# TensorE takes the six row products of a convolution two at a time, between the three chunks of direct rows

## The chip, the cores and the metric

The kernel runs on one core of a Trainium2 chip. The metric is the device time of one execution in microseconds (us); the kernel before has a median of 1493.2 us over 3 runs (1492.6 to 1494.61).

## What is computed

A residual block with batch normalisation over the whole batch, on 32 images of 128 channels and 56 x 56 pixels, in float32:

```python
residual = x
out = conv3x3_decomposed(x, lsq_quantize(w1, alpha1))
out = jax.nn.relu(batchnorm(out, gamma1, beta1))
out = conv3x3_decomposed(out, lsq_quantize(w2, alpha2))
out = batchnorm(out, gamma2, beta2)
out = jax.nn.relu(out + residual)
```

The convolutions are 3 x 3 with padding 1. `lsq_quantize` rounds the weights to integers from -4 to 3 times a scale. Mean and variance of a batch normalisation are taken over all images, so the second convolution can't start before the first has gone through all of them.

## The kernel before

**Phases.** The 128 channels lie on the 128 partitions. Phase 1 convolves the 32 images with w1 and sums their values and squares; phase 2 applies the first normalisation and ReLU, convolves with w2 and sums again; the last phase adds the residual, applies the second normalisation and ReLU and stores. Ten images fit in SBUF (`slots`); the others go out to HBM and come back. A step g is one image in phase 1 (g = 0 to 31) or phase 2 (g = 32 to 63).

**One image.** Output rows 0 to 35 are made by a Winograd scheme in the vertical direction: nine tiles of four rows, each from six sums of input rows. DVE makes these sums (`v_rows`, lines 619 to 639, by way of `q_rows` and `p_rows`), and they are split in a high and a low part (`v_hi`, `v_lo`), which TensorE multiplies one after the other. The six products of an image, here p0 to p5, are six matmuls of 512 columns each (line 855; three horizontal taps times two parts), each into a PSUM bank of its own (0 to 5). Output rows 36 to 55 are made directly: three chunks, here c0, c1 and c2, of 7, 7 and 6 rows, 18 matmuls each (line 875) of 398 columns in c0 and c1, and of 342 or 284 in c2. They read `d_hi` and `d_lo`, the two parts of the input rows from 35 on. c0 and c2 share PSUM bank 6, c1 has bank 7.

**The engines around TensorE, in the order of their own programs.** Every engine runs its instructions in the order written, and waits on semaphores.

- ACT, function `step` (line 497), for image g: `hi_direct` (462) makes `d_hi` of image g, once all three chunks of image g-1 are done, since they read the plane it writes; `take_chunk` (476) takes c2 of image g-1 out of PSUM; `take_m` (470) copies p0, then later p2 of image g; three squares (488) of image g-1; `hi_pairs` (457) makes `v_hi` of image g+1 in three pairs, pair k once p(2k+1) of image g is done (the wait in line 456); in phase 2 only, two ReLU instructions (494) on image g+2; `take_chunk` of c0 and of c1 of image g.
- DVE, function `step` (line 707): `make_qp(g+1)` (622, 623); `lo_direct` (648), which makes `d_lo` of image g from `d_hi`; `make_v(g+1)` (626 to 639); the sums of products (659 to 671) with `lo_of_pair(g+1, 0)` (643) among them; `rows_out` (673 to 692), whose row 3 waits for all six products; `add_totals` (697).
- POOL, `lo_of_pairs` (line 415): `v_lo` of pairs 1 and 2 (418), each when ACT has made its `v_hi`.
- TensorE, `convolve` (line 881): `products` waits for `v_lo` (lines 840, 844, 846) and for the DVE work that frees each bank. `chunk` waits, for c0, for `d_lo` of this image (line 866) and for all chunks of the image before to be out of PSUM (868); for c2, that c0 of this image is out of bank 6:

```python
if j == 2:
    pe.wait_ge(evac_done, g * NC + 1)
```

- SP issues loads and stores. At the end of phase 2 it also loads the first residual images into `xbuf`, the fourth and fifth (line 374 ff.) when the last image's six products are done, since their places hold what the products read.

`m_done` counts products, `chunk_done` chunks, `evac_done` chunks that are out of PSUM, `hi_ready` and `lo_ready` / `pool_lo_ready` the parts.

Of the kernel before, what the change touches and what calls it, by code (L numbers as in the profile page):

```python
# [27 lines left out]
def residual_block(nc, x, w1, alpha1, gamma1, beta1, w2, alpha2, gamma2, beta2, out):  # L28
# [13 lines left out]
    M = 6  # L42
# [34 lines left out]
    with ExitStack() as ctx:  # L77
# [131 lines left out]
        def run(plane, r0, r1, shift):  # L209
            at = LEAD + r0 * PITCH + shift  # L210
            return plane[:, at:at + run_length(r1 - r0)]

        def bank_run(bank, rows):
            return psum[:, bank, 0:run_length(rows)]
# [16 lines left out]
        def w_bank(k, h):  # L231
            return psum[:, W_BANK[k] + h, :].bitcast(BF16)
# [593 lines left out]
        @block.tensor  # L826
        def _(pe):
            def transpose_weights(k):
                pe.wait_ge(w_int_ready[k], 1)
                for h, (first, end) in enumerate(W_LOTS):  # L830
                    for t in range(first, end):
                        last = nc.tensor.transpose(w_bank(k, h)[:, (t - first) * C:(t - first + 1) * C],
                                                   w_int[k][:, t * C:(t + 1) * C], ident[:, :])
                    last.then_inc(transposed, 1)

            def products(g, w):
                first_step = isinstance(g, int) and g == 0
                for k in range(M):
                    if k == 0:
                        pe.wait_ge(lo_ready, g * LO + 1)  # L840
                        if not first_step:
                            pe.wait_ge(m_copied, g * 2 - 1)
                    if k == 2:
                        pe.wait_ge(pool_lo_ready, g * PLO + 1)
                    if k == 4:
                        pe.wait_ge(pool_lo_ready, g * PLO + 2)
                    if not first_step:

                        if k in (1, 2, 3):
                            pe.wait_ge(sums_ready, g * SR - (0, 4, 1, 0)[k])  # L850
                        if k in (4, 5):
                            pe.wait_ge(rows_ready, g * RR - (k - 4))
                    for kw in range(3):
                        for half in range(2):
                            last = nc.tensor.matmul(bank_run(M_BANK[k], TILES),  # L855
                                                    w[:, M_WEIGHT[k] + kw, :],
                                                    run(v_plane[half], k * TILES, (k + 1) * TILES, kw - 1),
                                                    start=(kw == 0 and half == 0), stop=(kw == 2 and half == 1))
                    last.then_inc(m_done, 1)


            taps = sorted(((kh, kw) for kh in range(3) for kw in range(3)), key=lambda t: t != (1, 1))

            def chunk(g, j, w):
                if j == 0:
                    pe.wait_ge(lo_ready, g * LO + LO)
                    if not (isinstance(g, int) and g == 0):
                        pe.wait_ge(evac_done, g * NC)
                if j == 2:
                    pe.wait_ge(evac_done, g * NC + 1)  # L870
                for n, (kh, kw) in enumerate(taps):
                    r0 = CHUNKS[j][0] + kh - 1
                    r1 = min(H, CHUNKS[j][1] + kh - 1)
                    for half in range(2):
                        last = nc.tensor.matmul(bank_run(CHUNK_BANK[j], r1 - r0),  # L875
                                                w[:, kh * 3 + kw, :],
                                                run(d_plane[half], r0 - WINO + 1, r1 - WINO + 1, kw - 1),
                                                start=(n == 0 and half == 0), stop=(n == TAPS - 1 and half == 1))
                last.then_inc(chunk_done, 1)

            def convolve(g, w):
                products(g, w)
                for j in range(NC):
                    chunk(g, j, w)

            pe.wait_ge(ident_ready, 1)
            transpose_weights(0)
            pe.wait_ge(wT_ready, 6)
            pe.wait_ge(pads_ready, PADS)
            for n in range(5):  # L890
                convolve(n, wT[0])
            pe.wait_ge(m_copied, 5 * 2)
            pe.wait_ge(sums_ready, 5 * SR - 1)
            transpose_weights(1)
            pe.wait_ge(wT_ready, 2 * 6)
            convolve(5, wT[0])
            with pe.Fori(3, IMAGES // 2) as i:
                for b in range(2):
                    convolve(i * 2 + b, wT[0])
            convolve(IMAGES, wT[1])  # L900
            convolve(IMAGES + 1, wT[1])
            with pe.Fori(IMAGES // 2 + 1, IMAGES) as i:
                for b in range(2):
                    convolve(i * 2 + b, wT[1])
# [21 lines left out]
```

## Time and profile before

| | |
|---|---|
| median of 3 runs | 1493.2 us (1492.6 to 1494.61) |
| profiled execution | 1492.18 us, of which the span is 1490.3 us |
| TensorE busy | 1134.6 us (76% of the span) |
| DVE busy | 1128.4 us (76%) |
| ACT busy | 854.7 us (57%) |
| POOL busy | 298.5 us (20%) |
| phase 1, first to last product | 24.0 to 587.2 us |
| phase 2, first to last product | 615.1 to 1169.8 us |
| last phase | from about 1187 us |

The span is from the first to the last instruction of one profiled execution; 1.9 us of its time lie outside it. Busy shares are means over three phases with different limits, so a stage has to be read by itself: how far one engine is from full in an image of phase 1 or 2, and which wait ends last there. A matmul's listed duration includes the time it takes to run through the array, so neighbouring rows overlap; what one costs is the distance of two starts.

### The profile page before, as it was taken

What the parts mean: (1) busy time and instruction counts of PE and PEld (TensorE: products, weight loads), DVE (VectorE), ACT (ScalarE), POOL (GpSimd) and SP (SyncE); (2) the same over time, 40 slices, a digit from 0 to 9 for tenths busy, and PEclk for the clock granted to TensorE, in tenths of its full rate; (3) what the DMA queues carried; (4) which work ended last, traced back from release to release, by engine and by line L of the source; (5) the groups of instructions that cost most, each with busy time, mean ns of one, the idle gap of its engine ahead of it and who ended that gap; (6) DMA issues with size and microseconds to landing.
All of it is one profiled execution on the core that took longest, in us unless ns stands there. A gap on an engine that the chain in (4) does not pass through costs nothing.

```text
span 1490.3 us, 18967 instructions
## 1 busy us (share of the span) xinstructions
PE 1134.6 (76%) x5802; PEld 1031.6 (69%) x5802; DVE 1128.4 (76%) x1626; ACT 854.7 (57%) x1263; POOL 298.5 (20%) x147
## 2 busy tenths in 40 slices
PE   3999999999999999599999999999999600000000
PEld 2998999999999999499999999999999600000000
DVE  7998888888888885798888888888888452322324
ACT  3555555555665554677777777777777352222234
POOL 3222222222222221322222222222222000000000
PEclk9999999999999999799999999999999855555555
DMA  4354555444442210022244555444230699999999
GB/s 164 135 197 151 193 188 195 190 172 172 172 179 108 101 43 0 1 87 87 86 172 183 194 188 195 188 172 172 86 129 33 231 414 431 430 429 429 430 430 408
DMA packets 28101, 296.88 MB, mean 199 GB/s; under 512 B 3888, under 2 KB 3888, under 8 KB 4784
## 3 DMA queue, kind: packets, MB, share of 16 engines
q1 hardware_dynamic: 22608, 245.25, 41.7%
q10 hardware_dynamic: 5472, 51.38, 8.1%
q8 instruction: 9, 0.15, 0.0%
q14 instruction: 12, 0.10, 0.0%
HBM read 174.59 MB, written 122.03 MB: 199 GB/s over the span
## 4 chain that ended last, share of the span: by engine, by line
issue 65%; DMA 17%; POOL 14%; DVE 1%; ACT 1%; POOLq 1%; ACTq 0%; DVEq 0%
POOL v_lo L418 14%; DMA slots<-conv_spill 11%; DMA out<-slots 4%; DMA xbuf<-in_x 3%; DVE slots L821 1%; ACT slots L576 1%; POOLq L423 0%; POOLq L417 0%; POOLq L77 0%; POOLq L418 0%; ACTq L580 0%; DVE tiny L748 0%; DVE affine L750 0%; DVE affine L751 0%; POOL ident L404 0%
## 5 line engine op out<-in xcount | busy, mean ns | idle before, releaser
L418 POOL TENSOR_TENSOR v_lo<-v_rows,v_hi 128x1008 fp32r<-128x1008 f32 x128 | 296.2, 2334 | 831.2 <-ACT v_hi L457 831.2
L875 PE MATMUL conv_psum<-d_hi,w1T 128*128 128x398 f32 (+2 forms) x864 | 284.6, 333 | 0.0
L875 PE MATMUL conv_psum<-d_hi,w2T 128*128 128x398 f32 (+2 forms) x864 | 284.6, 333 | 0.0
L875 PE MATMUL conv_psum<-d_lo,w1T 128*128 128x398 f32 (+2 forms) x864 | 283.3, 332 | 0.0
L875 PE MATMUL conv_psum<-d_lo,w2T 128*128 128x398 f32 (+2 forms) x864 | 283.3, 332 | 0.0
L855 PE MATMUL conv_psum<-v_hi,w2T 128*128 128x512 f32 x576 | 227.9, 396 | 18.3 <-DVE v_lo L643 18.3
L855 PE MATMUL conv_psum<-v_hi,w1T 128*128 128x512 f32 x576 | 229.2, 398 | 10.4 <-DVE v_lo L643 5.5
L488 ACT ACTIVATE squares<-slots,minus_shift 128x1008 bf16 (+3 forms) x192 | 225.0, 1172 | 8.4 <-ACT squares L488 2.9
L855 PE MATMUL conv_psum<-v_lo,w1T 128*128 128x512 f32 x576 | 229.2, 398 | 0.0
L855 PE MATMUL conv_psum<-v_lo,w2T 128*128 128x512 f32 x576 | 228.2, 396 | 0.0
L821 DVE SCALAR_TENSOR_TENSOR slots<-slots,affine,xbuf 128x3136 f32<-128x3136 f32 (+1 forms) x30 | 97.4, 3265 | 151.1 <-DMA slots<-conv_spill 146.9
L576 ACT ACTIVATE slots<-slots,affine 128x3136 f32<-128x3136 f32 (+1 forms) x34 | 93.6, 2754 | 202.8 <-DVE slots L821 202.0
L476 ACT ACTIVATE slots<-conv_psum 128x392 f32 (+3 forms) x192 | 91.5, 476 | 194.9 <-PE conv_psum L875 194.9
L457 ACT CAST v_hi<-v_rows 128x1008 fp32r<-128x1008 f32 x192 | 185.9, 1029 | 9.6 <-DVE v_rows L630 6.5
L648 DVE TENSOR_TENSOR d_lo<-slots,d_hi 128x1176 fp32r<-128x1176 f32 x64 | 88.6, 1385 | 125.1 <-ACT d_hi L462 125.1
L875 PEld LDWEIGHTS conv_psum<-d_lo,w1T 128*128 128x128 f32 x864 | 162.8, 188 | 1.3
L875 PEld LDWEIGHTS conv_psum<-d_lo,w2T 128*128 128x128 f32 x864 | 162.8, 188 | 1.3
L875 PEld LDWEIGHTS conv_psum<-d_hi,w2T 128*128 128x128 f32 x864 | 162.4, 188 | 1.4
L875 PEld LDWEIGHTS conv_psum<-d_hi,w1T 128*128 128x128 f32 x864 | 162.4, 188 | 1.3
L462 ACT CAST d_hi<-slots 128x1176 fp32r (+1 forms) x64 | 75.5, 1180 | 131.4 <-PE conv_psum L875 131.4
L606 DVE SCALAR_TENSOR_TENSOR q_rows<-slots 128x2016 f32 (+1 forms) x64 | 144.2, 2253 | 4.2 <-ACT slots L494 4.2
L855 PEld LDWEIGHTS conv_psum<-v_hi,w2T 128*128 128x128 f32 x576 | 109.1, 189 | 42.2 <-DVE v_lo L643 18.5
(75 smaller groups left out, 1509.0 us busy)
## 6 DMA issues: line engine op xcount, KB each, us to landing
conv_spill<-slots SPq DMA_DIRECT2D x44, 1568.0 KB, 6.1
slots<-conv_spill SPq DMA_DIRECT2D x44, 1568.0 KB, 10.9
slots<-in_x SPq DMA_DIRECT2D x31, 1568.0 KB, 8.9
out<-slots ACTq DMA_DIRECT2D x30, 1568.0 KB, 11.5
xbuf<-in_x SPq DMA_DIRECT2D x28, 1568.0 KB, 52.1
xbuf_w<-in_x SPq DMA_DIRECT2D x4, 1568.0 KB, 51.9
out<-slots ACTq DMA_DIRECT2D x4, 784.0 KB, 10.8
slots<-in_L_conv_w SPq DMA_DIRECT2D x2, 576.0 KB, 9.8
```

What stands on the lines that cost most here:

```text
L418: nc.gpsimd.tensor_tensor(pair_window(1, k), pair_rows(k), pair_window(0, k).bitcast(F32), ALU.subtract).then_inc(pool_lo_ready, 1)
L457: nc.scalar.copy(pair_window(0, k), pair_rows(k)).then_inc(hi_ready, 1)
L462: nc.scalar.copy(window(d_plane[0], 0, D_ROWS), rows_of(slot(p + SLOTS, WINO - 1))).then_inc(hi_ready, 1)
L476: nc.scalar.activation(rows_of(slot(p + SLOTS, r0, r1)), bank_rows(CHUNK_BANK[j], r1 - r0), ACT.Identity, accum_out=sums[b][:, col:col + 1 ...
L488: nc.scalar.activation(squares[:, 0:(r1 - r0) * W], slot(p + SLOTS, r0, r1), ACT.Square, bias=minus_shift[:, phase:phase + 1], accum_out=s ...
L576: nc.scalar.activation(z, z, ACT.Relu, bias=affine[:, 1, 1:2]).then_inc(final_ready, 1)
L606: return nc.vector.scalar_tensor_tensor(out=out, in0=in0, scalar=scalar, in1=in1, op0=ALU.mult, op1=ALU.add)
L648: nc.vector.tensor_tensor(window(d_plane[1], 0, D_ROWS), rows_of(slot(p, WINO - 1)), window(d_plane[0], 0, D_ROWS).bitcast(F32), ALU.subtr ...
L821: nc.vector.scalar_tensor_tensor(out=z, in0=z, scalar=affine[:, 1, 0:1], in1=xbuf[b][:, r0 * W:r1 * W], op0=ALU.mult, op1=ALU.add).then_in ...
L855: last = nc.tensor.matmul(bank_run(M_BANK[k], TILES), w[:, M_WEIGHT[k] + kw, :], run(v_plane[half], k * TILES, (k + 1) * TILES, kw - 1), s ...
L875: last = nc.tensor.matmul(bank_run(CHUNK_BANK[j], r1 - r0), w[:, kh * 3 + kw, :], run(d_plane[half], r0 - WINO + 1, r1 - WINO + 1, kw - 1) ...
```

## The change

TensorE no longer makes p0 to p5 and then c0, c1, c2, but p0, p1, c0, p2, p3, c1, p4, p5, c2. The number of instructions is the same, and so is every wait; `products` takes the list of those it makes. The programs of DVE, ACT, POOL and SP are unchanged.

```diff
-            def products(g, w):
+            def products(g, w, which):
                 first_step = isinstance(g, int) and g == 0
-                for k in range(M):
+                for k in which:
...
             def convolve(g, w):
-                products(g, w)
                 for j in range(NC):
+                    products(g, w, (2 * j, 2 * j + 1))
                     chunk(g, j, w)
```

**Into c2, on TensorE, in image 1.** Semaphores stand in brackets; `v_hi` and `v_lo` are operands of the products, `d_hi` and `d_lo` those of the chunks. Before, c2 (342 columns) follows c1 (398 columns):

```order
L875 MATMUL conv_psum<-d_hi,w1T 128x398
L875 MATMUL conv_psum<-d_lo,w1T 128x398
L875 MATMUL conv_psum<-d_hi,w1T 128x342 [waits evac_done]
L875 MATMUL conv_psum<-d_lo,w1T 128x342
L875 MATMUL conv_psum<-d_hi,w1T 128x342
```

Now it follows p5, whose matmuls have 512 columns:

```order
L855 MATMUL conv_psum<-v_hi,w1T 128x512 [waits rows_ready]
L855 MATMUL conv_psum<-v_lo,w1T 128x512
L855 MATMUL conv_psum<-v_hi,w1T 128x512
L855 MATMUL conv_psum<-v_lo,w1T 128x512
L855 MATMUL conv_psum<-v_hi,w1T 128x512
L855 MATMUL conv_psum<-v_lo,w1T 128x512
L875 MATMUL conv_psum<-d_hi,w1T 128x342 [waits evac_done]
L875 MATMUL conv_psum<-d_lo,w1T 128x342
```

Between c1 and c2 stand two products that were far ahead of both.

**Into c0, on TensorE, in image 1.** Before, p5 is what comes ahead of c0:

```order
L855 MATMUL conv_psum<-v_hi,w1T 128x512 [waits rows_ready]
L855 MATMUL conv_psum<-v_lo,w1T 128x512
L855 MATMUL conv_psum<-v_hi,w1T 128x512
L855 MATMUL conv_psum<-v_lo,w1T 128x512
L855 MATMUL conv_psum<-v_hi,w1T 128x512
L855 MATMUL conv_psum<-v_lo,w1T 128x512
L875 MATMUL conv_psum<-d_hi,w1T 128x398 [waits evac_done,lo_ready]
```

Now it is p1 (its wait is on `sums_ready`):

```order
L855 MATMUL conv_psum<-v_hi,w1T 128x512 [waits sums_ready]
L855 MATMUL conv_psum<-v_lo,w1T 128x512
L855 MATMUL conv_psum<-v_hi,w1T 128x512
L855 MATMUL conv_psum<-v_lo,w1T 128x512
L855 MATMUL conv_psum<-v_hi,w1T 128x512
L855 MATMUL conv_psum<-v_lo,w1T 128x512
L875 MATMUL conv_psum<-d_hi,w1T 128x398 [waits evac_done,lo_ready]
```

Of the six products of an image, two stand ahead of c0 now.

**ACT in phase 2, before and after alike.** `v_hi` is `hi_pairs`, `slots<-slots,affine` the ReLUs, `slots,sums<-conv_psum` the chunks taken out of PSUM:

```order
L457 CAST v_hi<-v_rows 128x18x56 [waits m_done,v_ready] x3
L494 ACTIVATE slots<-slots,affine 128x2072
L494 ACTIVATE slots<-slots,affine 128x1064
L476 ACTIVATE slots,sums<-conv_psum 128x392 [waits chunk_done] x2
L462 CAST d_hi<-slots 128x21x56 [waits chunk_done,relu_ready]
```

Nothing moves here; the instructions that feed c0 and c2 stand behind those that wait for p5.

## Rows read from the trace of the kernel before

**Rows 1.** Busy time by engine, one image in phase 1 and one in phase 2.
```profile
core 0: us, PE busy (x) PEld busy (x) DVE busy (x) ACT busy (x) POOL busy (x), PEclk, DMA share, GB/s
300.00:317.57 17.57, 17.57 (x91) 16.00 (x91) 15.35 (x25) 10.21 (x19) 4.42 (x2) 1.00 0.49 183
900.00:917.57 17.57, 17.57 (x91) 16.00 (x91) 15.41 (x25) 13.23 (x21) 4.43 (x2) 1.00 0.48 183
```

**Rows 2.** Timeline of TensorE, phase 1: start us, us, what. Starts of c1, c2, p0 and next c0.
```profile
309.60 0.35 PE L875 MATMUL conv_psum<-d_hi,w1T 128*128 128x398 f32 x1
...
312.86 0.32 PE L875 MATMUL conv_psum<-d_hi,w1T 128*128 128x342 f32 x1
...
315.54 0.39 PE L855 MATMUL conv_psum<-v_hi,w1T 128*128 128x512 f32 x1
...
323.88 0.35 PE L875 MATMUL conv_psum<-d_hi,w1T 128*128 128x398 f32 x1
```

**Rows 3.** Timeline of ACT, the same image of phase 1.
```profile
305.30 2.89 ACT L457 CAST v_hi<-v_rows 128x1008 fp32r<-128x1008 f32 x3
309.89 0.50 ACT L476 ACTIVATE slots<-conv_psum 128x392 f32 x1 [1.69 <-PE conv_psum L875]
310.28 0.19 ACT L476 ACTIVATION_READ_ACCUMULATOR slots<-conv_psum 128x1 f32 x1
...
315.89 1.18 ACT L462 CAST d_hi<-slots 128x1176 fp32r x1 [2.15 <-PE conv_psum L875]
```

**Rows 4.** Timeline of ACT, an image of phase 2.
```profile
908.32 3.28 ACT L494 ACTIVATE slots<-slots,affine  x2
911.50 0.47 ACT L476 ACTIVATE slots<-conv_psum 128x392 f32 x1
```

**Rows 5.** Timeline of DVE, phase 1: the image's end, then `make_qp` and `lo_direct`.
```profile
311.06 0.68 DVE L678 SCALAR_TENSOR_TENSOR slots<-conv_psum,s 128x504 f32 x1
...
311.74 2.25 DVE L606 SCALAR_TENSOR_TENSOR q_rows<-slots 128x2016 f32 x1
313.91 1.20 DVE L623 TENSOR_TENSOR p_rows<-slots 128x1008 f32 x1
317.28 1.39 DVE L648 TENSOR_TENSOR d_lo<-slots,d_hi 128x1176 fp32r<-128x1176 f32 x1 [2.17 <-ACT d_hi L462]
```

**Rows 6.** Timeline of POOL, the same image.
```profile
307.34 4.42 POOL L418 TENSOR_TENSOR v_lo<-v_rows,v_hi 128x1008 fp32r<-128x1008 f32 x2 [13.06 <-ACT v_hi L457]
```

**Rows 7.** Timeline of all engines, first images: DVE beside POOL; POOL's second follows.
```profile
31.77 3.12 DVE L606 SCALAR_TENSOR_TENSOR v_rows<-p_rows 128x504 f32<-128x504 f32 x2 [2.12 <-POOL v_lo L418]
...
37.53 2.19 POOL L418 TENSOR_TENSOR v_lo<-v_rows,v_hi 128x1008 fp32r<-128x1008 f32 x1 [3.77 <-ACT v_hi L457]
37.70 3.09 DVE L643 TENSOR_TENSOR v_lo<-v_rows,v_hi 128x1008 fp32r<-128x1008 f32 x1
```

**Rows 8.** Timeline of TensorE in the first image: p2 after its wait.
```profile
31.72 0.50 PE L855 MATMUL conv_psum<-v_hi,w1T 128*128 128x512 f32 x1 [2.45 <-POOL v_lo L418]
...
35.67 0.42 PE L855 MATMUL conv_psum<-v_hi,w1T 128*128 128x512 f32 x1
```

**Rows 9.** Timeline of TensorE, the first products of phase 2.
```profile
615.07 0.79 PE L855 MATMUL conv_psum<-v_hi,w2T 128*128 128x512 f32 x1 [18.30 <-DVE v_lo L643]
...
619.46 0.39 PE L855 MATMUL conv_psum<-v_hi,w2T 128*128 128x512 f32 x1
```

**Rows 10.** Granted clock (PEclk) in one microsecond of it, columns as in rows 1.
```profile
33.00:34.00 1.00, 1.00 (x4) 0.71 (x4) 1.00 (x1) 0.00 (x0) 0.76 (x1) 0.50 0.00 0
```

**Rows 11.** Groups of DVE by line and shape, images 2 to 5: the second weights.
```profile
L251 DVE SCALAR_TENSOR_TENSOR slots<-slots 128x384 bf16<-128x384 bf16 x6 | 3.3, 557 | 0.2
L241 DVE TENSOR_SCALAR slots<-slots 128x1152 bf16<-128x1152 f32 x1 | 2.8, 2808 | 0.0
```

**Rows 12.** Busy time around the end of phase 2, columns as in rows 1.
```profile
1185.00:1195.00 10.00, 0.00 (x0) 0.00 (x0) 9.26 (x13) 3.46 (x2) 0.55 (x1) 0.50 0.68 257
1200.00:1210.00 10.00, 0.00 (x0) 0.00 (x0) 8.00 (x3) 8.54 (x4) 0.00 (x0) 0.50 1.00 418
```

## The prediction, made before the changed kernel ran

> **What bounds the kernel now.** I read the waits of TensorE first, then busy time by engine for one image of each convolution phase, then the timelines of one image, and last the windows at the end of phase 2. In steady state TensorE is busy for the whole 17.57 us of an image, in both phases, at a granted clock of 1.00 [rows 1]; DVE has 2.2 us to spare, ACT 7.4 us in phase 1 and 4.3 us in phase 2. So the bound is TensorE, and there is no wait of it that a new order could remove, save one of 2.45 us in the first image [rows 8]. What an order can do is to uncover waits.
>
> The starts of the blocks give their costs at full clock [rows 2]: c1 312.86 - 309.60 = 3.26 us, c0, of the same shape, as much, c2 2.68, six products 323.88 - 315.54 = 8.34, or 2.78 for two. These stay the same, 17.54 us in all; only the waits of c0 and c2 are new questions.
>
> **The wait of c2.** It needs c0 out of PSUM. ACT takes c0 out behind `hi_pairs`, whose third pair waits for p5 of the same image, because p4 and p5 read the plane that it overwrites. Before, p5 was done 3.3 us before c0 was. Now p5 stands right ahead of c2, so c2 waits for a chain that begins when p5 ends. Counted from the end of p5:
>
> - TensorE's end to ACT's start 0.29 (c0 ended at 309.60, ACT began at 309.89 [rows 2, 3]).
> - third pair of `v_hi`: a third of 2.89, less the overlap, 0.93 [rows 3].
> - in phase 2 the two ReLUs, 911.50 - 908.32 = 3.18 [rows 4].
> - c0 out of PSUM: 310.28 - 309.89 + 0.19 = 0.58 [rows 3], and 0.08 back to TensorE. That last step is in no row of a binding wait; the shortest handover seen is 0.02 to 0.08 us (ACT's second pair to POOL [rows 3, 6]), the longest 0.35 (TensorE to `hi_direct`: c2 ended 315.54, ACT began 315.89). I take the low one, and keep 0.35 for the range.
>
> So TensorE idles 0.29 + 0.93 + 0.58 + 0.08 = 1.9 us before c2 in phase 1 and 1.9 + 3.2 = 5.1 us in phase 2. Before, this was nothing: ACT had done all of it during c0.
>
> **The wait of c0.** It needs `d_lo` of its image: `hi_direct` on ACT waits for c2 of the image before, then `lo_direct` on DVE. Before, 8.34 us of products covered it; now 2.78 us. By ACT's path, from the end of c2: 0.35 + 1.18 + 0.21 (317.07 to 317.28) + 1.39 = 3.1 us [rows 3, 5], 0.35 more than the cover. By DVE's own order there is a second path, from the end of p5: row 3 and row 0 of `rows_out` come after p5, and then `make_qp` stands ahead of `lo_direct`. Alone that is 0.3 + 1.2 + 0.1 + 3.3 + 1.4 = 6.3 us, less than the 1.9 + 2.68 + 3.1 = 7.7 of ACT's path. But POOL now makes the third pair's `v_lo` just then, from 0.29 + 1.03 + 0.08 = 1.4 to 3.6 us (4.42 / 2 each [rows 6]), and DVE's instructions with two inputs from SBUF wait for it: one of 1008 elements, which takes 1.20 [rows 5], took 3.09 us beside POOL's, nearly all of POOL's 2.19 us on top, and two of 504, which take at most 0.68 each, took 3.12 together [rows 7]. The sums out of PSUM kept to 0.68 us beside POOL [rows 5, 6], so those are not held. With `make_qp` held to 3.6, c0 can start at 3.6 + 2.17 + 1.12 + 1.39 = 8.3 us after p5 in phase 1. TensorE has its 1.9 + 2.68 + 2.78 = 7.36 us behind it by then and idles 0.9 us more. In phase 2 that second path is short of ACT's 5.1 + 2.68 + 3.1 = 10.9 us and hides; 0.35 us remains.
>
> The Trainium skill says the same of this pair (SBUF — State Buffer, "Who interferes with whom"): DVE with two SBUF inputs and GpSimd share a port pair that is held for a whole instruction, the second one blocking. The rows above agree, and carry the term.
>
> An image then takes 17.57 + 1.9 + 0.9 = 20.4 us in phase 1 and 17.57 + 5.1 + 0.35 = 23.0 in phase 2, without the clock.
>
> **The clock.** After the 2.45 us wait of the first image the granted clock fell to 0.50, its lower level of 1.2 GHz, soon after work began again [rows 8, 10]: the ten matmul steps of 512 columns from 31.72 to 35.67 us took 3.95 us where ten take 8.34 / 36 x 10 = 2.32, a loss of 1.6. After the 18.3 us gap before phase 2, ten took 619.46 - 615.07 = 4.39 us, a loss of 2.1 [rows 9]. The 5.1 us gap of phase 2 lies between these two, so I price each at 1.8, with 1.6 and 2.1 as ends, and 0 should the clock hold. The 1.9 us gap of phase 1 is shorter than any in the trace that the clock fell behind: its price is between 0 and 1.6, and 0.9 us of that would go into the new wait of c0. I take 0.2, for a fall in some of the images.
>
> The Trainium skill has a rule that differs (TensorE: Matmul & The Clock Gate, "Why this matters for your kernels"): idle gaps up to about 3 us don't cost the clock. By it the 2.45 us gap should not have, and it did. By that rule phase 1 would lose nothing, and the sum would be 31 x 0.2 = 6 us lower; for phase 2 rule and row agree.
>
> **The ends.** In the first image c0 now stands ahead of p2 and fills the 2.45 us wait, which also saves the slow stretch behind it: -4. The second weights are prepared on DVE between images 2 to 5: 2.8 and 3.3 us [rows 11] and two instructions of 0.8. DVE's spare time took them in before; with `make_qp` on the path they come in nearly whole: +7 (0 and 7.7 are the ends). Images 0, 32 and the last of each phase have no wait of one kind or the other: 31 waits of each kind a phase, and in phase 2 the ReLUs are in 30 of these. At the end of phase 2, residual loads 4 and 5 are issued when p5 of the last image is done, now 2.7 us before TensorE's end instead of 9.2. They are 3.2 MB, 7.7 us at 418 GB/s, and the DMA engines, full from there to the end, had 0.32 x 10 = 3.2 us free [rows 12]: 0 to +4.5, and I take 2. The loads and stores within the phases take 49% of the DMA engines [rows 1] and hide.
>
> **Sum**, against the profiled execution (1492.18 us; the median of the runs is 1.0 higher): phase 1, 31 x (20.4 + 0.2 - 17.57) = 31 x 3.0 = 93; phase 2, 30 x (23.0 + 1.8 - 17.57) = 30 x 7.2 = 216, and one image without ReLUs 3; start +3; end +2. 1492 + 93 + 216 + 3 + 3 + 2 = **1809 us**.
>
> **Rivals.**
>
> - *The clock holds.* For it: in steady state TensorE works over three quarters of each image. Against: the fall after 2.45 us. Time 1492 + 31 x 2.85 + 30 x 5.4 + 3 + 5 = 1750 us.
> - *POOL holds DVE up less, or not.* If `totals` and `q_rows` get ahead of POOL's instruction, only 0.35 us of the 0.9 is left: 31 x 0.55 = 17 less, 1792. Against: POOL's instruction is released 0.2 us before DVE's.
> - *The clock falls behind every gap at full price, and the handover is long.* Phase 1: 20.4 + 0.6 + 0.27; phase 2: 23.0 + 2.1 + 0.27. 1492 + 31 x 3.7 + 30 x 7.8 + 8 = 1849 us.
> - *Not slower: the waits fall away.* If ACT could take c0 out while TensorE makes p2 to p5 (6 us for 0.58 of work), c2 would not wait; and if `d_lo` were made from rows ready before c2 ends, neither would c0. Then only the first image changes, 1492 - 4 = 1488 us. This decides only if both waits are under 0.1 us an image; `hi_pairs` stands ahead of `take_chunk` in ACT's written order and waits on p5 itself, so nothing speaks for it. Likewise for "nothing changes".
>
> **How the numbers follow.** The forecast has 0.55, holding clock 0.15, less of POOL 0.15, full price 0.12, not slower 0.03. A measurement here tells 0.2% (3 us) from no change. The range goes from 1750, the holding clock, to 1845, just short of the full price: about 0.85 by these cases, and errors of 0.2 us in a handover, over 62 images, are 12 us and inside it. Faster 0.015, same 0.01, slower 0.975.
>
> **What would show it.** TensorE's busy time about the same or higher (slow matmuls); idle before L875 of some 1.9 us x 31 and 5.1 us x 31, released by ACT L476, and before c0 of 0.9 and 0.35, released by DVE L648; ACT L457 newly waiting for TensorE; the distance of images 20.4 to 20.6 and 24.8; DVE L697 or L606 drawn out beside POOL L418 in phase 1; PEclk below 1 in phase 2 and near 1 in phase 1. It is wrong if c2 doesn't wait for ACT, if an image of phase 1 takes under 19 us, or if the clock in phase 2 stays at 1.00.

## The result, and the profile after

The changed kernel takes **1821.6 us** (median of 4 runs, 1820.16 to 1823.79) against 1493.6 us before (4 runs, 1492.6 to 1494.61): 1.220 times as long, 95% interval 1.2185 to 1.2214. The prediction was 1809 us, in a range of 1750 to 1845. The profiled execution took 1823.79 us, of which 1822.0 are the span.

One image of phase 1 and three of phase 2, by the windows of the changed kernel's trace, in the columns of [rows 1]:

```profile
414.45:434.93 20.48, 18.08 (x91) 15.82 (x91) 16.62 (x25) 10.09 (x18) 4.44 (x2) 1.00 0.41 157
1000.00:1075.15 75.15, 59.99 (x272) 53.14 (x272) 50.64 (x73) 39.88 (x62) 13.22 (x6) 0.89 0.33 128
```

Before, TensorE was busy for 17.57 of 17.57 us. Now an image takes 20.48 us in phase 1, with the granted clock at 1.00, and 75.15 / 3 = 25.05 us in phase 2, with it at 0.89 on average. TensorE's three largest waits over the whole run (engine, line, waited for: total us, times, longest):

```profile
PE conv_psum L875 <- ACT slots L476: 198.2, 62, 4.8
PE conv_psum L875 <- DVE d_lo L648: 37.8, 48, 4.1
PE conv_psum L855 <- DVE v_lo L643: 23.8, 2, 18.3
```

The first is c2's wait for c0 to be out of PSUM, once in each of the 62 images in which the prediction had it; the second is c0's wait for `d_lo`. Neither existed before. The third is as it was.

**Phase 1, one turn.** TensorE's two waits, then ACT, DVE and POOL between them (start us, us, what, idle time before):

```profile
408.01 0.42 PE L875 MATMUL conv_psum<-d_hi,w1T 128*128 128x342 f32 x1 [1.66 <-ACT slots L476]
...
414.45 0.44 PE L875 MATMUL conv_psum<-d_hi,w1T 128*128 128x398 f32 x1 [0.73 <-DVE d_lo L648]
```

```profile
406.44 1.03 ACT L457 CAST v_hi<-v_rows 128x1008 fp32r<-128x1008 f32 x1 [2.58 <-PE conv_psum L855]
407.38 0.49 ACT L476 ACTIVATE slots<-conv_psum 128x392 f32 x1
407.77 0.19 ACT L476 ACTIVATION_READ_ACCUMULATOR slots<-conv_psum 128x1 f32 x1
...
411.12 1.18 ACT L462 CAST d_hi<-slots 128x1176 fp32r x1 [2.68 <-PE conv_psum L875]
```

```profile
408.26 1.47 DVE L697 TENSOR_TENSOR totals<-totals,sums 128x10 f32<-128x10 f32 x1
409.65 2.25 DVE L606 SCALAR_TENSOR_TENSOR q_rows<-slots 128x2016 f32 x1
411.82 1.20 DVE L623 TENSOR_TENSOR p_rows<-slots 128x1008 f32 x1
412.94 1.37 DVE L648 TENSOR_TENSOR d_lo<-slots,d_hi 128x1176 fp32r<-128x1176 f32 x1
```

```profile
407.55 2.15 POOL L418 TENSOR_TENSOR v_lo<-v_rows,v_hi 128x1008 fp32r<-128x1008 f32 x1 [1.33 <-ACT v_hi L457]
```

The three casts of `hi_pairs`, which ran as one block of 2.89 us in [rows 3], are split: the third waits 2.58 us for p5, and c0's way out of PSUM (407.38, done at 407.96) stands right behind it. c2 starts 0.05 us later. Then the second wait: `d_hi` is ready at 412.30, but DVE starts `lo_direct` only at 412.94, with no idle time before it. It is late because `totals`, ten elements that took 0.17 us in every image before, takes 1.47: it starts at 408.26 and ends with POOL's instruction, at 409.7. So of the two paths to c0 it is DVE's that binds in phase 1, as the prediction had it. From the end of POOL's instruction on, `q_rows`, `p_rows` and `lo_direct` follow one another without a gap.

**Phase 2, one turn.** The ReLUs come in between:

```profile
1042.00 0.65 PE L875 MATMUL conv_psum<-d_hi,w2T 128*128 128x342 f32 x1 [4.83 <-ACT slots L476]
1049.30 0.45 PE L875 MATMUL conv_psum<-d_hi,w2T 128*128 128x398 f32 x1 [0.32 <-DVE d_lo L648]
```

```profile
1037.26 1.03 ACT L457 CAST v_hi<-v_rows 128x1008 fp32r<-128x1008 f32 x1 [2.58 <-PE conv_psum L855]
1038.20 3.28 ACT L494 ACTIVATE slots<-slots,affine  x2
1041.38 0.47 ACT L476 ACTIVATE slots<-conv_psum 128x392 f32 x1
```

c2 waits 4.83 us, and starts slowly: its first matmul is listed with 0.65 us where it is 0.42 in phase 1. The granted clock of 0.89 over three images is a mean of its two levels, 2.4 and 1.2 GHz; part of what follows c2's wait runs at the lower one (0.50 from 1042 to 1044 us, 1.00 again from 1045 to 1049).

### The profile page after: what moved, and what is told of

Read it like the earlier page. It is cut to its first block, busy times and chain, and to the rows that moved or that the text cites. A ratio compares the mean times of both kernels' runs of the same rounds, so it can differ in the third digit from the quotient of the medians.

```text
span 1822.0 us, 18967 instructions
## 1 busy us (share of the span) xinstructions
PE 1231.2 (68%) x5802; PEld 1084.9 (60%) x5802; DVE 1206.8 (66%) x1626; ACT 849.7 (47%) x1263; POOL 293.0 (16%) x147
## 4 chain that ended last, share of the span: by engine, by line
issue 74%; DMA 14%; POOL 8%; DVE 1%; ACT 1%; POOLq 0%; ACTq 0%; DVEq 0%
DMA slots<-conv_spill 9%; POOL v_lo L418 8%; DMA out<-slots 3%; DMA xbuf<-in_x 3%; DVE slots L821 1%; ACT slots L576 1%; POOLq L423 0%; POOLq L417 0%; POOLq L418 0%; POOLq L77 0%; ACTq L580 0%; DVE tiny L748 0%; DVE affine L751 0%; DVE affine L750 0%; POOL ident L404 0%
## 5 line engine op out<-in xcount | busy, mean ns | idle before, releaser
L418 POOL TENSOR_TENSOR v_lo<-v_rows,v_hi 128x1008 fp32r<-128x1008 f32 x128 | 290.7, 2272 | 1172.2 <-ACT v_hi L457 1172.2
L875 PE MATMUL conv_psum<-d_hi,w2T 128*128 128x398 f32 (+2 forms) x864 | 331.0, 384 | 156.1 <-ACT slots L476 146.6
L875 PE MATMUL conv_psum<-d_hi,w1T 128*128 128x398 f32 (+2 forms) x864 | 293.9, 344 | 80.2 <-ACT slots L476 51.6
L875 PE MATMUL conv_psum<-d_lo,w2T 128*128 128x398 f32 (+2 forms) x864 | 320.4, 373 | 0.0
L875 PEld LDWEIGHTS conv_psum<-d_hi,w2T 128*128 128x128 f32 x864 | 194.4, 225 | 184.2 <-ACT slots L476 159.7
L457 ACT CAST v_hi<-v_rows 128x1008 fp32r<-128x1008 f32 x192 | 191.5, 1028 | 167.9 <-PE conv_psum L855 163.7
L470 ACT COPY m<-conv_psum 128x504 f32<-128x504 f32 x128 | 73.6, 575 | 329.6 <-PE conv_psum L855 329.6
L875 PEld LDWEIGHTS conv_psum<-d_lo,w2T 128*128 128x128 f32 x864 | 194.7, 225 | 1.5
L643 DVE TENSOR_TENSOR v_lo<-v_rows,v_hi 128x1008 fp32r<-128x1008 f32 x64 | 77.8, 1215 | 116.6 <-ACT v_hi L457 116.6
## 6 DMA issues: line engine op xcount, KB each, us to landing
out<-slots ACTq DMA_DIRECT2D x4, 784.0 KB, 10.3
```

The lines of the kernel that those rows point to most:

```text
L418: nc.gpsimd.tensor_tensor(pair_window(1, k), pair_rows(k), pair_window(0, k).bitcast(F32), ALU.subtract).then_inc(pool_lo_ready, 1)
L457: nc.scalar.copy(pair_window(0, k), pair_rows(k)).then_inc(hi_ready, 1)
L470: nc.scalar.copy(rows_of((m1, m3)[j][:, :]), bank_rows(M_BANK[2 * j], TILES)).then_inc(m_copied, 1)
L643: nc.vector.tensor_tensor(pair_window(1, k), pair_rows(k), pair_window(0, k).bitcast(F32), ALU.subtract).then_inc(lo_ready, 1)
L875: last = nc.tensor.matmul(bank_run(CHUNK_BANK[j], r1 - r0), w[:, kh * 3 + kw, :], run(d_plane[half], r0 - WINO + 1, r1 - WINO + 1, kw - 1) ...
```

## The experiments

The changed kernel gives two waits, a collision and a clock. Ten kernels took these apart; the times are compared with 1492 to 1494 us for the kernel before, run beside them. "An image" is the distance of two images in the trace, read from the starts of `d_hi` or `d_lo`.

### c0_out_early: what stands between p5 and c2 on ACT is taken away

```diff
-                    hi_pairs(g + 1)
+                    hi_pairs(g + 1, (0, 1))
+                take_chunk(g, p, b, 0)
+                if not last:
+                    hi_pairs(g + 1, (2,))
                 if relu_next is not None:
                     relu_next()
-                for j in range(NC - 1):
-                    take_chunk(g, p, b, j)
+                take_chunk(g, p, b, 1)
```

> The changed kernel, with ACT taking c0 out of PSUM ahead of the third pair of v_hi (and of the ReLUs) instead of behind them. My theory: the wait of c2 goes in both phases (ACT is free 3 us before p5 ends), but DVE's path stays, since it starts at p5 too: POOL's instruction, make_qp, lo_direct, 8.3 us from p5 to c0, with 5.5 us of TensorE's work in it. So an image takes 17.57 + 2.9 = 20.4 us in phase 1, no less than now, and 20.4 in phase 2 instead of 25.05: 1821 - 31 x 0 - 30 x 4.6 = about 1680 us, up to 1700 if the clock falls behind the 2.9 us wait of c0. Rival (ACT's hi_direct chain is the only other wait): an image takes 17.9 us in both, 1821 - 31 x 2.6 - 30 x 7.1 = 1525 us.

Measured: 1731.8 us (ratio 1.161, 1.154 to 1.168), 32 us beyond my upper end. An image takes 20.49 us in phase 1 and 22.2 in phase 2. All waits of c2 are gone; within both phases TensorE waits for nothing but `d_lo`. One such wait of each phase:

```profile
419.07 0.45 PE L877 MATMUL conv_psum<-d_hi,w1T 128*128 128x398 f32 x1 [2.66 <-DVE d_lo L650]
```

```profile
943.43 0.70 PE L877 MATMUL conv_psum<-d_hi,w2T 128*128 128x398 f32 x1 [2.91 <-DVE d_lo L650]
```

An image of phase 1 did not gain a hundredth of a microsecond from losing 1.7 us of wait: c0's wait took it all, as DVE's path from p5 demands. The rival's 1525 us is out. Phase 2 came out 1.8 us an image above the 20.4 expected: the granted clock there is 0.92 against 1.00 in phase 1, and c0's matmuls, behind the wait, take 4.92 us (921.16 to 926.08) where they take 3.38 in phase 1 (419.07 to 422.45).

### c0_moved_alone and c2_moved_alone: each half of the change

```diff
             def convolve(g, w):
-                for j in range(NC):
-                    products(g, w, (2 * j, 2 * j + 1))
-                    chunk(g, j, w)
+                products(g, w, (0, 1))
+                chunk(g, 0, w)
+                products(g, w, (2, 3, 4, 5))
+                chunk(g, 1, w)
+                chunk(g, 2, w)
```

> Half of the change: p0, p1, c0, then p2 to p5, c1, c2. c1 (3.26 us) then stands between p5 and c2 again. My theory: in phase 1 c2 does not wait (its chain is 1.9 us), in phase 2 it waits 5.1 - 3.3 = 1.8 us or a little more; c0 waits 0.35 us by ACT's path, up to 1.7 where DVE, which finishes its sums after p5 and p3 later than before, is behind. 19.2 us an image in phase 1 at most (17.9 at least), 20.3 in phase 2, 1492 - 4 + 31 x 1.7 + 30 x 2.8 = 1624 us, at least 1583, and up to 1650 with a falling clock. Rival (the price is that of switching between products and chunks, of any kind): two thirds of the changed kernel's loss stay, about 1710 us.

Measured: 1649.7 us (ratio 1.106, 1.103 to 1.109). An image takes 19.2 us in phase 1, where only c0 waits (1.4 us each, for `d_lo`), and 20.55 in phase 2, where c2 waits 2.2 us. The waits over the whole run:

```profile
PE conv_psum L875 <- ACT slots L476: 64.2, 30, 2.2
PE conv_psum L875 <- DVE d_lo L648: 60.5, 57, 4.7
```

The time is at my upper end of 1650, but not for the falling clock that I had put there: it is at 1.00 from 300 to 500 us and at 0.99 from 900 to 1200. Images 0 to 5 alone came 17.3 us later than in the kernel before.

The second half of the change:

```diff
-                for j in range(NC):
-                    products(g, w, (2 * j, 2 * j + 1))
-                    chunk(g, j, w)
+                products(g, w, (0, 1, 2, 3))
+                chunk(g, 0, w)
+                chunk(g, 1, w)
+                products(g, w, (4, 5))
+                chunk(g, 2, w)
```

> The other half: p0 to p3, c0, c1, p4, p5, c2. c0 has 5.56 us of products ahead of it again, more than ACT's path (3.1 us) and than DVE's (8.3 from p5, where TensorE now has 1.9 + 2.68 + 5.56 = 10.1 us). My theory: c0 does not wait, c2 waits 1.9 us in phase 1 and 5.1 in phase 2 as in the changed kernel, so an image takes 19.45 us in phase 1 (the clock holds) and 22.6 plus the clock's 2.0 = 24.7 in phase 2: 1492 + 31 x 1.9 + 30 x 7.1 + 5 = 1769 us. If the clock's fall depends on where its periods meet the gap, phase 1 may lose up to 1 us an image more: 1800. Rival (c0's position is the costlier one): below 1650 us.

Measured: 1764.1 us (ratio 1.183, 1.178 to 1.187). c2 waits as in the changed kernel, to the tenth, and c0 hardly at all:

```profile
PE conv_psum L875 <- ACT slots L476: 198.2, 62, 4.8
PE conv_psum L855 <- DVE v_lo L643: 23.8, 2, 18.3
PE conv_psum L832 <- DVE slots L251: 16.2, 1, 16.2
PE conv_psum L855 <- POOL v_lo L418: 2.8, 1, 2.8
PE conv_psum L875 <- DVE d_lo L648: 2.6, 3, 1.3
```

An image takes 19.48 us in phase 1, which is 17.57 + 1.9, and 24.4 in phase 2. So the two halves cost 272 (c2) and 158 us (c0) by themselves and 328 together: they don't add. In phase 1 c0 waits 1.4 us by itself and 0.73 behind c2's wait, which hides part of the time in which `d_lo` is made. In phase 2 the c0 half has 2.2 us of c2's wait in it, and that is part of the same 4.8. The rivals, a price of switching and c0 as the costlier half, are both out.

### gap_filled: the clock apart from the wait

```diff
+            def filler(g, w):
+                pe.wait_ge(m_copied, g * 2 + 1)
+                for _ in range(20):
+                    nc.tensor.matmul(bank_run(M_BANK[0], TILES), w[:, 0, :],
+                                     w[:, 0:4, :].rearrange("c t o -> c (t o)"), start=True, stop=True)
...
                     products(g, w, (2 * j, 2 * j + 1))
+                    if fill and j == NC - 1:
+                        filler(g, w)
                     chunk(g, j, w)
```

> The changed kernel with 20 extra matmuls of 512 columns ahead of c2 in the 31 images of phase 2 that wait there (images 32 to 61), 20 x 0.232 = 4.64 us of work into bank 0, which is free by then; their result is not used. They fill the 5.1 us wait and take none of what c2 waits for. My theory (the wait of c2 is 5.1 us, and the slow stretches behind it cost about 2.1 more): the clock stays at 1.00 in phase 2 and an image takes 23.0 us instead of 25.05, 1821 - 30 x 2.05 = 1760 us although TensorE does 139 us more of matmuls. Rival (the clock's fall lies in the gap and costs next to nothing, and the waits are longer than I count): no gain, 1815 to 1825 us.

Measured: 1768.7 us (ratio 1.186, 1.182 to 1.189). TensorE does 20 matmuls more in each of 30 images and the kernel is 53 us faster than the changed one. Its windows, phase 1 and phase 2:

```profile
300.00:500.00 200.00, 176.16 (x880) 154.01 (x879) 164.81 (x238) 98.09 (x175) 44.30 (x20) 1.00 0.42 161
900.00:1200.00 300.00, 292.30 (x1422) 252.78 (x1421) 217.39 (x308) 171.94 (x260) 56.24 (x26) 1.00 0.36 136
```

The clock stays at 1.00, and an image of phase 2 takes 23.24 us instead of 25.05. The slow stretches therefore cost 1.8 us an image; the waits, with the slower first matmuls behind them, cost 23.24 - 17.57 = 5.7, not 5.4. (The text of the expectation speaks of 31 images and then names 32 to 61, which are 30; 30 have the filler.)

### relus_behind_chunks: the ReLUs alone

```diff
-                if relu_next is not None:
-                    relu_next()
                 for j in range(NC - 1):
                     take_chunk(g, p, b, j)
+                if relu_next is not None:
+                    relu_next()
```

> The changed kernel, with ACT's two ReLUs of phase 2 behind its taking c0 and c1 out of PSUM instead of ahead. My theory: c2 waits 1.9 us in phase 2 as in phase 1; the ReLUs then delay q_rows, so c0 waits 1.9 us too, and an image takes 21.3 us if the clock holds behind these two, and up to 23.3 if it falls: 1821 - 30 x 3.75 = 1709 us, up to 1770. Phase 1 is unchanged at 20.48. Rival (c2's wait in phase 2 is not the ReLUs but a general slowness of ACT there): above 1790 us.

Measured: 1747.3 us (ratio 1.170, 1.168 to 1.172). Phase 1 is at 20.48 us; in phase 2 images take 21.7 or 23.2 us, in turn or two of the longer in a row. TensorE's waits in phase 2, 900 to 1200 us:

```profile
PE conv_psum L875 <- DVE d_lo L648: 27.1, 14, 2.0
PE conv_psum L875 <- ACT slots L476: 21.6, 13, 1.7
```

c2's longest wait is phase 1's 1.7 us, and c0's is the 2.0 that the moved ReLUs put on `q_rows`. The price lies between the 1709 us of a holding clock and the 1770 of a falling one, which fits the granted clock of 0.95 there.

### pool_pair2_small and qp_ahead_of_rows: the collision of POOL and DVE

The first leaves the order alone and cuts POOL's second instruction of an image to one row; the low part of the last two sums is zero but for one row.

```diff
-                    nc.gpsimd.tensor_tensor(pair_window(1, k), pair_rows(k), pair_window(0, k).bitcast(F32),
-                                            ALU.subtract).then_inc(pool_lo_ready, 1)
+                    n = 2 * TILES if k == 1 else 1
+                    nc.gpsimd.tensor_tensor(pair_window(1, k)[:, 0:n, :], pair_rows(k)[:, 0:n, :],
+                                            pair_window(0, k).bitcast(F32)[:, 0:n, :],
+                                            ALU.subtract).then_inc(pool_lo_ready, 1)
```

> The changed kernel, with POOL's second instruction of an image cut from 18 rows to one: the low part of the last pair of sums is zero but for one row, so outputs differ. Nothing in DVE's order changes. My theory: DVE's totals and q_rows are held only by that instruction (totals takes 1.44 us instead of 0.17), so c0's wait in phase 1 falls to ACT's 0.35 us and an image to 19.8 us; phase 2 stays: 1821 - 31 x 0.7 = 1799 us. Rival (DVE's own order, rows 3 and 0 and make_qp behind p5, is what is late): 20.48 us an image, 1821 us.

Measured: 1798.9 us (ratio 1.204, 1.202 to 1.207). `totals` is back at 0.16 us, c0 waits 0.3 us in phase 1 and an image there takes 20.0 us; phase 2 has 25.0 us an image, as in the changed kernel.

```profile
412.77 0.16 DVE L700 TENSOR_TENSOR totals<-totals,sums 128x10 f32<-128x10 f32 x1
412.86 2.25 DVE L609 SCALAR_TENSOR_TENSOR q_rows<-slots 128x2016 f32 x1
```

The mechanism is as expected, but that the time met the forecast of 1799 us is luck. An image of phase 1 gained 0.45 us and not 0.7, while images 0 to 5, which the forecast took for images like the others, came 10.3 us earlier (the `d_hi` of image 6 starts at 155.14 instead of 165.47 us), and the first image of phase 2 takes 26.27 us instead of 29.75. POOL's instruction did more harm in those places than in the steady state.

The second leaves POOL alone and moves DVE's work ahead of its wait for p5:

```diff
+                if between is not None:
+                    between()
+                    make_qp(g + 2, p + 2)
                 dve.wait_ge(m_done, g * M + M)
                 dve.wait_ge(sums_ready, g * SR + 5)
                 row(3, m5, 1.0, d)
...
-                if input_ready is not None:
-                    input_ready()
-                    make_qp(g + 1, p + 1)
                 lo_direct(g, p)
```

> The changed kernel, with DVE making q_rows and p_rows of the image after next ahead of rows 3 and 0, so ahead of its wait for p5, instead of behind them. My theory: DVE's path from p5 to c0 is what makes c0 wait 0.7 to 0.9 us in phase 1; without it ACT's path is left, 0.35 us more than its cover. Phase 1 goes from 20.48 to 19.8 us an image and phase 2 stays at 25.05: 1821 - 31 x 0.7 = 1799 us. Rival (c0's wait in phase 1 is ACT's as in phase 2, only longer): both phases as they are, 1821 us.

Measured: 1850.7 us (ratio 1.239, 1.237 to 1.241), 29 us **more** than the changed kernel, and 52 more than my own expectation. An image of phase 1 takes 21.2 us, and c0 waits 1.46 us there. DVE and POOL there:

```profile
356.84 2.25 DVE L606 SCALAR_TENSOR_TENSOR q_rows<-slots 128x2016 f32 x1
359.00 3.15 DVE L623 TENSOR_TENSOR p_rows<-slots 128x1008 f32 x1
```

```profile
357.22 3.87 POOL L418 TENSOR_TENSOR v_lo<-v_rows,v_hi 128x1008 fp32r<-128x1008 f32 x1 [1.21 <-ACT v_hi L457]
```

`q_rows` has begun when POOL's instruction is released, so POOL stands still until 359.0 and then does its 2.1 us, and `p_rows` stands still until that is over at 361.1. In these rows, as in those of the changed kernel, the instruction that began first is not slowed and the other waits until it is over: 1.8 us are lost once on POOL and 1.95 on DVE. I had moved the pair into the same collision from its other side. The Trainium skill (SBUF — State Buffer, "Who interferes with whom") says so in as many words: "Issue order, not op shape, decides who blocks."

### qp_ahead_pool_small and relus_ahead_of_pair3: was it the collision?

The first is the last two edits together.

> Both of qp_ahead_of_rows and pool_pair2_small: q_rows and p_rows ahead of rows 3 and 0, and POOL's second instruction of an image cut to one row (the low part of the last pair of sums is zero but for that row). In qp_ahead_of_rows alone phase 1 got longer, 21.15 us an image instead of 19.8, and I put that down to q_rows now starting just before POOL's instruction: POOL took 3.9 us instead of 2.2 and p_rows 3.15 instead of 1.2. My theory: with POOL's instruction small that goes, c0 waits 0.3 us in phase 1, and an image takes 20.0 us as in pool_pair2_small: 1821 - 31 x 0.5 = 1800 us with phase 2 unchanged. Rival (the new order of DVE itself is slow, since rows 3 and 0 come later): 21.1 us an image and 1850 us.

Measured: 1804.9 us (ratio 1.209, 1.205 to 1.213); an image of phase 1 takes 20.07 us and c0 waits 0.3. In phase 1 DVE's new order is harmless without POOL beside it. The 6 us more than in pool_pair2_small lie mostly in phase 2 (776.65 us from the first `d_hi` to the last, against 770.81), and were not taken apart.

The second starts from c0_out_early:

```diff
-                if not last:
-                    hi_pairs(g + 1, (2,))
                 if relu_next is not None:
                     relu_next()
+                if not last:
+                    hi_pairs(g + 1, (2,))
                 take_chunk(g, p, b, 1)
```

> c0_out_early with the ReLUs of phase 2 moved ahead of the third pair of v_hi. Phase 1 is unchanged at 20.49. In phase 2 the ReLUs no longer stand between p5 and anything. My theory: the third pair then comes about 1 us later (the ReLUs end at 13.5 us after c0's start, p5 at 12.1), POOL's instruction runs from 14.6 to 16.8 us and q_rows wants to start at 14.5, so the two collide in full, whichever is first: c0 of the next image at 21.4 us, where it is 20.4 in c0_out_early without the clock. So the period of phase 2 does not fall below 21.4 us, and with slow stretches behind a wait of 3.5 us it is 22 to 23.5: 1725 to 1775 us against 1732. Rival (POOL and DVE do not hold each other up here): 19.3 us an image in phase 2, and 1645 us.

Measured: 1780.0 us (ratio 1.192, 1.188 to 1.196), 5 us beyond my upper end and 48 above c0_out_early, for an edit that takes 3.2 us of ReLUs out of the chain. An image of phase 2 takes 23.9 us. The collision is there in full:

```profile
969.57 2.25 DVE L608 SCALAR_TENSOR_TENSOR q_rows<-slots 128x2016 f32 x1
971.74 3.14 DVE L625 TENSOR_TENSOR p_rows<-slots 128x1008 f32 x1
```

```profile
969.75 4.06 POOL L418 TENSOR_TENSOR v_lo<-v_rows,v_hi 128x1008 fp32r<-128x1008 f32 x1 [2.29 <-ACT v_hi L457]
```

It and the clock (0.85 there) make up the 23.9. By the starts of TensorE's matmuls c0 waits 3.4 us (972.87 to 976.31), and its own matmuls take 6.13 us (976.31 to 982.44) for 3.26, which is 2.9 more.

### first_image_alone: what is worth keeping of the change

On the kernel before:

```diff
-            for n in range(5):
+            products(0, wT[0], (0, 1))
+            chunk(0, 0, wT[0])
+            products(0, wT[0], (2, 3, 4, 5))
+            chunk(0, 1, wT[0])
+            chunk(0, 2, wT[0])
+            for n in range(1, 5):
                 convolve(n, wT[0])
```

> The kernel before with one change: in image 0 TensorE makes p0, p1, c0, then p2 to p5, c1, c2; all others as before. My theory: c0 fills the 2.45 us wait for POOL and the slow stretch behind it does not come, 4 us, and the images after it are bound by TensorE as before: 1492 - 4 = 1488 us. Rival (the first images are bound by DVE, which was 98% busy from 80 to 100 us and whose work starts no earlier): 1491 to 1493 us.

Measured: **1487.7 us** (5 runs, 1487.58 to 1488.21) against 1494.15: ratio 0.9961, 0.9947 to 0.9974. It is faster than both kernels, by 0.4% than the one before. c0 is ready when p1 ends and runs in the place of the 2.45 us wait of [rows 8]; the clock is at 1.00 where it was 0.50 in [rows 10]:

```profile
28.71 0.34 PE L875 MATMUL conv_psum<-d_hi,w1T 128*128 128x398 f32 x1
```

```profile
29.00:33.00 4.00, 4.00 (x23) 3.83 (x22) 1.84 (x3) 0.00 (x0) 4.00 (x2) 1.00 0.00 0
33.00:36.00 3.00, 3.00 (x15) 2.42 (x14) 3.00 (x3) 2.42 (x3) 0.84 (x1) 1.00 0.00 0
```

The spans differ by 4.3 us, what the wait and the slow stretch were worth; the rest of the difference of the medians lies within the spread of the runs before.

## Why the prediction was right

Point by point, from the starts of `hi_direct` in both traces (image 0 at 23.73 us in each):

- **What bounds it.** TensorE was full in the images of both phases. The wait of the first image was worth the predicted 4 us, by first_image_alone (4.3 us of the span).
- **The wait of c2.** Predicted 1.9 us in phase 1 and 5.1 in phase 2. By the matmul starts it is 408.01 - 406.19 = 1.8 in phase 1 (the last start of p5 was 405.96, plus 0.23 for it) and 1042.00 - 1037.01 = 5.0 in phase 2; the waits listed are 1.66 and 4.83, where the matmul before is counted longer. c2_moved_alone gives 19.48 - 17.57 = 1.9 by the distance of images. The handover from ACT to TensorE that no row had shown, 0.08 us by the low bound, is 0.05.
- **The wait of c0.** Predicted 0.9 in phase 1 by DVE's path with POOL's hold, 0.35 in phase 2 by ACT's; listed 0.73 and 0.32, and by the starts 0.9 and 0.47. The hold was argued from two rows ahead of the run; pool_pair2_small and the pair of runs after it show it: without POOL's instruction c0 waits 0.3.
- **Images of phase 1.** 20.48 us against 20.6. The clock was at 1.00 in the steady images (300 to 500 us), so the 0.2 us put in for it were 0. Images 6 to 30 came 72.7 us later, 2.91 each: 1.8 and 0.9 of wait, and 0.2 of slower first matmuls behind the two waits (c0 takes 3.37 us from its first start to that of p2, and 3.26 in [rows 2]).
- **The start.** Images 0 to 5 came 165.47 - 140.23 = 25.2 us later, 7.8 beyond six times 2.91, against the net +3 predicted. The first image did save (45.53 - 23.73 = 21.8 us for it against 24.64), but images 2 to 5 came 25.4 us later, 13.7 beyond four times 2.91 where the second weights take 7.7, and the clock fell there too (0.91 from 60 to 145 us). In pool_pair2_small images 0 to 5 end 10.3 us earlier, at a clock of 0.98 from 60 to 145 us; six times its gain of an image, 0.45, is only 2.7. So POOL's hold has a large share of the excess, directly or by the clock; the split between the two was not tried. Phase 1 with its start was predicted at +96 and came to 677.14 - 579.24 = 97.9. That this is so near is luck: some 6 us of clock that were not lost stand against 5 at the start and 2 to 3 in the images.
- **Images of phase 2.** Predicted +219, came to 330.1 - 98.1 = 232 from `hi_direct` of image 32 to that of image 63. This is the term that was mis-sized. The clock's 1.8 us an image was right, by gap_filled. The waits were 5.7 instead of 5.4 us an image (23.24 - 17.57): 30 x 0.25 = 7.5. It was not c2's chain that was too short (5.0 us by the starts for 5.1), but c0's wait (0.47 for 0.35) and the slower first matmuls behind both waits, 0.2 us, for which the sum had no term. The other 5.6 are in the first image of phase 2 alone, which took 29.75 us for 16.9, 12.9 more where 7.2 were reckoned. The prediction gave this image no wait of c0, and it has one of 3.82 us, with a slow c0 behind it (5.87 us to the start of p2):

```profile
721.88 0.70 PE L875 MATMUL conv_psum<-d_hi,w2T 128*128 128x398 f32 x1 [3.82 <-DVE d_lo L648]
```

```profile
715.15 4.26 DVE L606 SCALAR_TENSOR_TENSOR q_rows<-slots 128x2016 f32<-128x2016 f32 x1 [2.00 <-ACT slots L494]
```

  The `q_rows` that stands ahead of this `d_lo` waited for a ReLU and then took 4.26 us for 2.25, beside POOL, whose instructions ran until 717.29. In pool_pair2_small it took 2.40 and c0 waited 1.46.
- **The end.** Predicted +2; from the last `hi_direct` to the end of the span it is 331.7 - 330.1 = 1.6 us.

Of the rivals, the holding clock was wrong in phase 2 and right in phase 1, which is why a forecast of one price for each phase came out near. The rule on idle gaps of about 3 us that the prediction quoted from the Trainium skill (TensorE: Matmul & The Clock Gate, "Why this matters for your kernels") held for the changed kernel, 1.7 us without a fall in phase 1 (300 to 500 us) and 4.8 with one in phase 2. c0_out_early lies at its edge: its waits of 2.9 us in phase 2, 3.1 by the matmul starts, came with a clock of 0.92.

## What to carry to other kernels

When work is interleaved on the engine that bounds, look at every instruction that another engine runs behind a wait for the moved piece: here ACT's third cast waited for p5, and c0's way out of PSUM stood behind it, so moving p5 by a few microseconds made a wait out of an order that was harmless. Follow each such wait round the whole loop before mending one: taking c2's wait away gave nothing in phase 1, because a second path from the same event ended 0.9 us later. And give an interleaving only to the place that has a wait to fill; in this kernel that was one image of 64, and 0.4% of the time.

## What was not expected of the hardware

- Two waits of almost one length had different effects on the clock. In c0_out_early, 2.66 us once in 20.49 us left the granted clock at 1.00 over 200 us of phase 1, and 2.91 us once in 22.2 us had it at 0.92 over 300 us of phase 2, at a cost of 22.2 - 20.49 = 1.7 us an image:

```profile
300.00:500.00 200.00, 174.39 (x881) 155.23 (x879) 161.85 (x235) 100.98 (x180) 44.34 (x20) 1.00 0.42 161
900.00:1200.00 300.00, 262.08 (x1224) 236.17 (x1223) 224.93 (x322) 176.31 (x269) 58.92 (x27) 0.92 0.37 142
```

  What tells them apart, the quarter of a microsecond or the distance of the waits, stays open; in the first image of the kernel before, a wait of only 2.45 us was followed by a fall. The length of a gap alone does not decide it. One difference is in the traces: in that first image TensorE's matmuls of 512 columns started 0.43 us apart up to the last one before the wait (28.43 and 28.86 us), the distance of the slow stretch behind it, where they are 0.23 apart in phase 1 of c0_out_early. Whether that matters was not tried.
- An instruction of ten elements can take 1.47 us: `totals` was held by a POOL instruction that had begun before it. A group's duration shows this at once (the median of L697 went from 0.17 to 1.44 us), while the list of waits shows nothing, since the time counts as busy.
